# Order of the transposes in the expert loops, and two small operations moved to other engines in the state-space stage

## What is computed

```python
h = _L0_tok_ref(x, ...)                             # 16 frames of a patch merged into 8
h = h + _L0_attn_ref(_layernorm(h, axis=-1), ...)   # state-space mixer
h = h + _L0_ffn_ref(_layernorm(h, axis=-1), ...)    # 8 experts, two for each token
h = h + _L1_attn_ref(_layernorm(h, axis=-1), ...)   # linear attention with a decay mask
h = h + _L1_ffn_ref(_layernorm(h, axis=-1), ...)    # 3 experts, one for each sequence of 32

# in the mixer, per token; norm_w scales the columns
y = jnp.moveaxis(ys, 0, 1) + D[None, None, :, None] * xs
yg = y * jax.nn.silu(z)
yn = yg * jax.lax.rsqrt(jnp.mean(jnp.square(yg), -1, keepdims=True) + EPS) * norm_w
return yn @ W_out

# an expert: 192 -> 768 -> 192
h = gelu(x @ w_up[e]); o = h @ w_down[e]
```

## Time and profile before

| what | us |
|---|---|
| median of 3 runs | 558.98 |
| lowest and highest run | 557.87, 562.82 |
| the profiled execution's own time | 562.9 |
| its span, first to last instruction | 561.0 |

### The profile page before, as it was taken

The page is one execution under the profiler, slowest core; times in us unless marked ns, Lnnn a source line. Parts: engine busy times, 40 slices in busy tenths (PEclk is TensorE's granted clock), DMA queues, the critical chain, the costliest instruction groups (busy, mean ns, idle before and its releaser), DMA issues.

```text
span 561.0 us, 15458 instructions
## 1 busy us (share of the span) xinstructions
PE 500.1 (89%) x5695; PEld 449.3 (80%) x5695; DVE 360.8 (64%) x999; ACT 260.7 (46%) x771; POOL 225.8 (40%) x316
## 2 busy tenths in 40 slices
PE   8999999999897058999999999999999997999993
PEld 7677768888786058889898889898888886998993
DVE  2576579989999584555555555554357665666661
ACT  2678868695566232222222222222457642453541
POOL 1255540016786333444444444432212214444422
PEclk9999989999999669999999999999999998999998
DMA  9992000008001101131221311210733323122110
GB/s 259 244 200 42 3 0 2 0 2 336 16 30 37 35 24 36 48 84 43 80 51 44 87 44 44 43 38 31 232 112 100 92 73 84 51 67 72 58 37 21
DMA packets 32379, 40.73 MB, mean 73 GB/s; under 512 B 7121, under 2 KB 27730, under 8 KB 32306
## 3 DMA queue, kind: packets, MB, share of 16 engines
q1 hardware_dynamic: 25586, 25.39, 16.7%
q0 software_dynamic: 5760, 12.98, 8.1%
q10 hardware_dynamic: 960, 1.38, 0.9%
HBM read 29.41 MB, written 10.32 MB: 71 GB/s over the span
## 4 chain that ended last, share of the span: by engine, by line
PE 48%; issue 5%; ACT 4%; another core or an unknown queue 4%; DVE 3%; POOLq 0%; DVEq 0%; POOL 0%; ACTq 0%
PE psum L1565 20%; PE psum L1577 14%; PE psum L1547 4%; PE psum L1956 3%; PE psum L1960 2%; PE psum L137 1%; PE psum L1967 1%; ACT hidden_room L1602 1%; ACT rows_turned L1915 1%; ACT rows_turned L1592 1%; PE psum L1713 1%; DVE hidden_room L1315 1%; PE psum L1948 1%; ACT hidden_room L1604 0%
## 5 line engine op out<-in xcount | busy, mean ns | idle before, releaser
L1565 PE MATMUL psum<-rows_turned,expert_weights 64*128 64x128 f32 x2052 | 130.6, 278 | 13.2 <-ACT rows_turned L1592 9.2
L1565 PEld LDWEIGHTS psum<-rows_turned,expert_weights 64*128 64x128 f32 x2052 | 122.8, 190 | 24.5 <-issue 24.2
L1577 PE MATMUL psum<-expert_second_weights,hidden_room 64*128 64x192 f32 x1368 | 125.4, 327 | 2.2 <-issue 2.2
L1577 PEld LDWEIGHTS psum<-expert_second_weights,hidden_room 64*128 64x128 f32 x1368 | 112.1, 187 | 2.7 <-issue 2.7
L1590 ACT ACTIVATE rows_turned<-psum 128x192 f32<-128x192 f32 x57 | 18.9, 331 | 181.5 <-PE psum L1547 151.7
L1529 POOL DMA_INDIRECT y<-rows_out,out_row_by_slot x39 | 45.7, 1171 | 90.2 <-DVE rows_out L1659 90.2
L1657 DVE COPY rows_out<-psum 128x192 f32<-128x192 f32 x39 | 14.0, 358 | 74.5 <-PE psum L1577 74.5
L1522 POOL DMA_INDIRECT rows_in<-x,token x39 | 42.9, 1099 | 22.4 <-issue 11.6
L855 PE MATMUL psum<-arena 97*128 97x512 f32 (+1 forms) x192 | 49.5, 417 | 0.5 <-ACT h L600 0.5
L855 PEld LDWEIGHTS psum<-arena 97*128 97x128 f32 (+1 forms) x192 | 37.8, 200 | 9.9 <-ACT h L600 0.9
L919 DVE SCALAR_TENSOR_TENSOR conv_out<-psum,param,conv_out 128x496 f32<-128x496 f32 (+2 forms) x60 | 41.9, 715 | 3.2 <-ACT conv_out L867 1.8
(11 more groups left out here) (284 smaller groups left out, 974.3 us busy)
## 6 DMA issues: line engine op xcount, KB each, us to landing
w_proj<-in_w_proj SPq DMA_DIRECT2D x8, 576.0 KB, 7.6
sz<-in_x SPq DMA_DIRECT2D x16, 192.0 KB, 7.9
w_fc<-in_w_fc SPq DMA_DIRECT2D x4, 768.0 KB, 18.7
w<-in_w SPq DMA_DIRECT2D x3, 576.0 KB, 4.1
w_fc<-in_w_fc SPq DMA_DIRECT2D x4, 384.0 KB, 17.0
x<-xf_tile SPq DMA_DIRECT2D x16, 96.0 KB, 1.6
expert_rows<-y SPq DMA_DIRECT2D x8, 192.0 KB, 4.1
hidden_room<-y SPq DMA_DIRECT2D x8, 192.0 KB, 4.6
```

Source lines behind the costliest of these rows:

```text
L1565: done = nc.tensor.matmul(ps_h[t.odd][half][:, ch, :], w_now[at, t.odd, first:first + P], xt[at, t.odd, block, :], start=block == 0 and ch ...
L1577: done = nc.tensor.matmul(ps_y[half], hid[at, t.odd, ch, :], w_down_now[at, t.odd, ch * D:(ch + 1) * D], start=ch == 0, stop=ch == HC - 1)
```

## The change

Three edits. (1) In the experts' TensorE step the transposes of the next tile come first: `turn_rows(s-1)`, `up(s-2)`, `down(s-3)`; every wait stays with its operation. (2) `mean_square` moves from VectorE to ScalarE, first in ScalarE's step, ahead of `decays`. (3) `set_shift` moves from VectorE to GpSimd, directly behind `roots` in the same step (before, VectorE did it one step later). VectorE's list is shorter by two, its other operations keep their order.

```diff
+        def mean_square(t):
+            if t.i < TILES:
+                act.wait_ge(q_mm, t.i + 1)
+                need(act, roots_done, t.i - 1)
+                act.activation(under[:, t.odd, 0:1], ps_q[t.odd], ACT.Identity, bias=c["eps"], scale=1.0 / DI).then_inc(ms_done, 1)
...
-        pipelined(act, TILES + MS_TO_VAR, [(2, decays), (6, with_eps), (5, squares), (3, skips), (7, norm)], 8, straight=True)
+        pipelined(act, TILES + MS_TO_VAR, [(6, mean_square), (2, decays), (6, with_eps), (5, squares), (3, skips), (7, norm)], 8, straight=True)
...
-        def mean_square(t):
-            dve.wait_ge(q_mm, t.i + 1)
-            need(dve, roots_done, t.i - 1)
-            nc.vector.tensor_scalar(under[:, t.odd, 0:1], ps_q[t.odd], 1.0 / DI, EPS, ALU.mult, ALU.add).then_inc(ms_done, 1)
-
...
-        def set_shift(t):
-            dve.wait_ge(roots_done, t.i + MS_TO_VAR + 1)
-            need(dve, xf_done, t.i - 1)
-            nc.vector.tensor_scalar(shift2[:, t.odd:t.odd + 1], mv[:, t.i % 4, 0:1], rms[:, t.i + MS_TO_VAR, 1:2], -1.0, ALU.mult, ALU.mult).then_inc(shift_set, 1)
-
-        pipelined(dve, TILES, [(2, mask_bc), (7, residual), (2, times_dt), (6, mean_square), (7, sum_rows), (2, mixing), (7, moments), (7, best), (4, add_skip), (9, set_shift), (7, best_index), (4, gate)], 10, straight=True)
+        pipelined(dve, TILES, [(2, mask_bc), (7, residual), (2, times_dt), (7, sum_rows), (2, mixing), (7, moments), (7, best), (4, add_skip), (7, best_index), (4, gate)], 8, straight=True)
...
+        def set_shift(t):
+            i = t.i - MS_TO_VAR
+            if i >= 0:
+                pool.wait_ge(roots_done, t.i + 1)
+                need(pool, xf_done, i - 1)
+                nc.gpsimd.tensor_scalar(shift2[:, i % 2:i % 2 + 1], mv[:, i % 4, 0:1], rms[:, t.i, 1:2], -1.0, ALU.mult, ALU.mult).then_inc(shift_set, 1)
...
-        pipelined(pool, TILES + MS_TO_VAR, [(0, spread), (5, sum_squares), (6, roots)], 7, straight=True)
+        pipelined(pool, TILES + MS_TO_VAR, [(0, spread), (5, sum_squares), (6, roots), (6, set_shift)], 7, straight=True)
...
-        pipelined(pe, n_tiles, [(2, up), (1, turn_rows), (3, down)], 4, straight=True)
+        pipelined(pe, n_tiles, [(1, turn_rows), (2, up), (3, down)], 4, straight=True)
```

## The result

| | before | after |
|---|---|---|
| median of the runs, us | 559.75 (4 runs) | 536.45 (4 runs) |
| lowest and highest, us | 557.87, 562.82 | 533.99, 539.03 |
| the profiled execution's own time, us | 562.9 | 533.99 |
| its span, us | 561.0 | 532.1 |

The ratio after to before is 0.9579, with a 95% interval of 0.9515 to 0.9643: faster by 4.2%, and 23.3 us between the medians. One more run of the kernel before went into this comparison than front and forecast had, so its median is 559.75 here. In each of these kernels a few executions take some per cent longer at a lower granted clock; the ratios and their intervals leave those out.

What follows compares the result with a forecast made beforehand. The experts' TensorE steps were taken as the bound, each losing 0.49 us to one wait; VectorE bounds the state-space stage. Gains of 24.2 + 3.4 = 27.6 us turn 558.98 into 531.4 us; range 526 to 543, the forecast's own 528 to 535.

Steps and rivals of the forecast that it cites:

- The bound and its mechanism: First experts: transposes first removes TensorE's wait for transposed rows, 0.49 us per step; steps go from 4.68 to 4.19 us.
- The slack for the rows: Experts' step: transposed rows, needed 4.19 us after the transposes begin, take 2.6 us with the late signal; 1.6 us spare.
- step (b): Experts' step: if the first product's signal is late instead, the gelu still ends 0.7 us before its `down`.
- the third rival: Experts: the order doesn't matter, the late signal moves along and steps stay at 4.68 us; 552 us, chance 0.04.
- The start of the first experts: Transposes and warm-up put the first product at 210.5, the second at 212.7 instead of 213.56; gain 0.9 us.
- The second experts: Second product 2.2 us after the first, then 16 steps of 4.19 at the 2.4 GHz level; gain 7.6 us.
- VectorE's list: State-space stage: VectorE's step loses two slots, 3.51 to 3.32 us; seven steady steps give 1.3 us.
- cushion: State-space stage: GpSimd's added shift is over its idle time by 0.1 us, taken up by its stretched second sum.
- The early steps and the drain: State-space stage: four slow early steps gain 1.0 us (0 to 1.7), its end 1.1; with 1.3 from steady steps, 3.4.
- The first rival, the slow pattern: State-space stage: GpSimd's later work meets `mixing` and `gate` every step, steps become 3.90 us; 539 us, chance 0.20.
- From the span to the median: Whole kernel: the 27.6 us taken off the profiled span of 561.0 carries over to the median, 558.98 to 531.4.

Runs made afterwards that it cites:

- ScalarE's longer work: Changed kernel with ScalarE reading each first half of the transposed rows twice more ahead of its eviction: 536.55 us, ratio 0.9585 to the kernel before.

## Why the prediction was right, point by point

**The bound and its mechanism: right.** The one wait of 0.49 us per step in the first experts is gone, the step is 4.20 us (4.19 forecast), and nothing else became late in it. The term was 15.7 + 0.9 = 16.6 us; measured are 16.2 (15.7 from the second product on, 0.5 at the start). The slack for the rows was worked out from the late signal of the earlier trace rows; in fact these rows now come in time, because the gather has another place against the transposes. That the first product's signal would be the late one was step (b): the gelu was put some 4 us behind the step's beginning, and starts 303.63 - 299.68 = 3.95 behind it in the latest case; in most steps it is 3.0. The 0.7 us left for its `down` were by the second experts' six pieces; the first experts' two leave 306.19 - 304.51 = 1.7.

**What the prediction missed:** the reason for the late signal. It said that no row told why. The rows did: the steps of the earlier trace rows, which it took only as proof of what TensorE can do, are the ones without a gather. It cost nothing here, but knowing it would have excluded the third rival, which had 0.04.

**The start of the first experts: mis-sized by 0.4 us.** The first product comes 1.4 us later after the last norm (205.13 - 182.53 = 22.60 against 209.40 - 188.17 = 21.23) where 1.1 were put. The second comes 2.30 behind it, where 2.2 were put.

**The second experts: 7.1 for 7.6 us, and that by luck.** Their second product was put at 2.2 us behind the first and came at 2.29; the third came 4.33 later, and five later steps are 4.23 to 4.29 instead of 4.19. I expected the level of 2.4 GHz throughout, and this execution had it. But of the six profiled executions with the transposes first (this one, the second one of the same kernel, the order alone, ScalarE's longer work, and the two without the warm-up) it is the only one that did. In the second execution of the same kernel:

```profile
448.73 4.21 PE L1568 MATMUL psum<-rows_turned,expert_weights 64*128 64x128 f32 x36
```

```profile
446.40:453.30 6.90, 6.66 (x56) 6.32 (x58) 2.46 (x5) 0.87 (x4) 2.58 (x3) 0.51 0.34 99
```

(The second row is of the table by windows: window, length, busy time of PE, PEld, DVE, ACT and POOL, granted clock, DMA share, GB/s.) The first product takes 4.21 us, not 2.28, and from the last product of the first experts to that of the second are 156.83 us, against 154.00 here; with the order alone and with ScalarE's longer work it is 155.61 and 155.59. So where the clock falls this stage gains 4.3 to 5.5 us. The prediction took it that without the idle time of 2.25 us of the earlier trace rows the clock would stay up; it fell behind two idle times of 1.6 to 1.8 and 0.9 to 1.2 us, with six transposes between them, and where it stayed up these were 1.65 and 1.01.

**VectorE's list: right.** 3.32 us were forecast, 3.32 are there. The mean square on ScalarE takes 0.26 us and finds its cover (0.93 us of wait left); the squares start 0.25 us into the step (about 0.3 forecast). The shift on GpSimd takes 0.27 us, not 0.34, and starts 0.10 behind the root's end. GpSimd's second sum is stretched still (1.16 us), and was not needed as a cushion: its five instructions of a step are 3.10 us of 3.32.

**The early steps and the drain: 3.9 for 3.4 us in all.** Of the 2.8 us between the mixings of tiles 5 and 15, seven steps of 0.19 are 1.3, so the early ones gave 1.5, where 1.0 was taken from a range of 0 to 1.7: none of them meets a sum any more. The drain gave its 1.1 in this execution (13.32 us for 14.45), and with the warm-up left out (13.31). In the four other profiled executions with both moves it is 14.04 to 14.23, a gain of 0.2 to 0.4.

**The first rival, the slow pattern: right about the danger, wrong about what brings it.** It needs GpSimd's sums to come early or late by 0.1 to 0.2 us. Edit 3 alone brings it, edit 2 alone brings a milder one, both together miss it narrowly: the first sum's recorded end is 0.03 us behind the mixing's start, and the second begins 0.11 behind it. The chance of 0.20 was fair; that it was missed was not something that my estimates, good to 0.1 us, could tell, and so was luck. The Trainium skill (page "SBUF — State Buffer", section "Who interferes with whom") says that whoever issues first blocks the other fully. The rows agree, less a constant: a sum that began 0.08 us before the mixing and takes 0.46 us prolonged it by 0.24 us, where 0.38 were left of the sum; one that began 0.17 us before it prolonged it by 0.15, where 0.29 were left. Each time the one behind pays what is left of the other less 0.14 us.

**From the span to the median: the weak step.** The sum was 27.6 us and the spans differ by 28.9, of which 1.8 are not of the change: 27.1 against 27.6. But the medians differ by 23.3, so 531.4 was 5 us low. The 536.45 measured lie in the stated 526 to 543, but outside the forecast's own 528 to 535, which is wider already than its terms make it: with the early steps and the drain at nothing or in full they give 530.7 to 533.5. I carried the difference of one execution over to the median. Parts of the kernel that the change doesn't touch vary by more than that between executions: the first mixing starts at 122.80 us with the order alone, at 126.67 with the mean square alone, at 131.88 with the shift alone, and the last had 13.7 us of half clock from 29.8 on:

```profile
29.00:44.00 15.00, 15.00 (x114) 11.22 (x113) 7.28 (x34) 7.44 (x24) 5.99 (x18) 0.54 1.09 199
```

(That is the table by windows of the kernel with the shift alone.) Of the kernel before, the profiled execution was the slowest shown; of the one after, it was the fastest of four, and the second profiled execution of it has a span of 535.8 us, 3.7 more, with the same steps of 4.20: 2.8 of these lie in the second experts, where the clock fell, and 0.9 in the drain. With 4.3 to 5.5 us for the second experts and 0.2 to 0.4 for the drain, the 27.1 become 23.4 to 24.8, which fits the 23.3 of the medians. So the terms of the steps were right, and those of the second experts and of the drain were sized for the best case. That the executions without a profile ran like this is likely, not shown.

## What to carry to other kernels

A consumer that must wait for a late signal is cured by distance: put the producer's operation ahead of another long one, so that the consumer's product is a whole step away. Cost a stall by the steps that don't have it, and ask what those steps lack: here it was a gather. And where engines share a path, a slot of 0.1 us taken off one list is worth nothing until one has looked where it moves the neighbours' instructions: two edits that gained nothing gained 3.7 us together.

## What I had not expected of the hardware

- **An indirect DMA on GpSimd delays TensorE's signals.** With a gather on GpSimd at that place, ScalarE takes the transposed rows 1.33 to 1.54 us behind their recorded end, which is 0.26 to 0.51 us behind the gather's end (31 steps of the kernel before); with a scatter alone 0.38 to 0.46 us in nearly all steps; with the transposes last, when the gather has been over for 1.6 us, at 0.00 us. It isn't that simple everywhere: in the changed kernel the gelu starts at 303.63, 0.22 us before the gather's recorded end, and in the kernel before the very first rows are taken without delay at 208.64 with a gather recorded from 208.12 to 209.64. What exactly holds the signal was not tried.
- **Whoever comes second pays what is left of the other, less 0.14 us.** A sum already under way for 0.08 us costs it 0.24 us, one under way for 0.17 costs 0.15; what was left of the sums was 0.38 and 0.29. A sum that begins 0.11 us behind the mixing, with 0.84 us of it left, costs the mixing nothing and is itself prolonged by 0.70, from 0.46 to 1.16 us. The root of 1.42 us under the mixing (0.70 alone, with 0.86 left) and the shift of 0.68 us beside the gate (0.27 alone, with 0.54 left, its recorded start 0.01 us ahead of the gate's) fit the same sum within 0.01 us.
- **The clock falls in some executions and not in others, at the same idle time.** Behind 1.0 us of idle time at the start of the second experts it was at full speed in one execution of the changed kernel and at 0.51 from 446.4 to 453.3 us in another, with the warm-up in both. Half clock was the rule there: five of the six profiled executions with the new order had it, and their first product took 2.87 to 4.21 us instead of 2.28.
